# Second cross-attention: scores as 32-row tiles of one head instead of a block-diagonal query, and a BF16 one-hot spread in the expert layer

## The chip, the cores and the metric

The kernel runs on one core of a Trainium2 chip. A core has TensorE (matmuls into PSUM, eight banks of 512 fp32 columns), VectorE, ScalarE, GpSimd, and SyncE, whose queue here issues every DMA. The metric is device time in microseconds of one execution of the whole program, lower is better. TensorE's clock is granted by a throttle: 1.00 in the profile is 2.4 GHz, 0.50 is 1.2 GHz.

## What is computed

Two layers act on x (2 batches, 128 tokens, 128 features); each step is a layer norm, an operation and a residual. Layer 0 has a 16-head cross-attention on a context of 2048 keys, a latent attention and a top-1 expert layer of 8 experts; layer 1 a sparse cross-attention on the same context, a self-attention and a 16-expert layer. The change touches the expert layer of layer 0 and the cross-attention of layer 1:

```python
def _L0_ffn_ref(hidden_states, Wr, br, W1, W2):
    x = hidden_states.reshape(-1, h)
    route = jax.nn.sigmoid(x @ Wr + br)
    max_prob = jnp.max(route, axis=1, keepdims=True)
    max_ind = jnp.argmax(route, axis=1)
    for e in range(n_experts):
        mask = (max_ind == e)[:, None].astype(x.dtype)
        y = jax.nn.gelu(x @ W1[e], approximate=False) @ W2[e]
        out = out + mask * y
    out = out * max_prob

def _L1_xattn_ref(iQ, iK, mask, Wq, Wkv, Wo, nbias):
    rq = (iQ @ Wq.T).reshape(b, q, H, ADIM)          # 16 heads of 8
    kv = (iK @ Wkv.T).reshape(b, s, 2, H, ADIM)
    rk, rv = (kv[:, :, 0], kv[:, :, 1])
    scores = jnp.einsum('bqhd,bshd->bhqs', rq, rk) / sqrt(ADIM)
    scores = jnp.where(mask[:, None, :, :], jnp.float32(-1e+32), scores)
    t = jax.nn.relu(scores + nbias[0])
    t = t * t
    attn = t / (t.sum(-1, keepdims=True) + IEPS)
    o = jnp.einsum('bhqs,bshd->bqhd', attn, rv).reshape(b, q, H * ADIM)
    return o @ Wo.T
```

## The kernel before

Everything is written out by hand, engine by engine: each engine's program is a list of instructions in a fixed order, and semaphores tie the lists together. Names of semaphores say what is done (`mo_proj`: latent attention projected, `kstack_in[i]`: stacked keys of one group landed).

*Keys and values of layer 1* are projected early, in gaps: `fill(gap)` issues the items that `FILL` lists for a gap, "k" items (512 keys) and "v" items (four fp32 matmuls of 128 columns for 512 keys); ScalarE copies each out of its bank (`FILL_BANK`). fill(5), after the router's matmul, holds v1 to v7.

*Expert layer.* VectorE makes a one-hot of the chosen expert, then `diag`, 128x1024 per batch: identity times one-hot. TensorE multiplies xn with it (L889, four fp32 matmuls of 512 columns), which gives x laid out per expert with zeros elsewhere; ScalarE and VectorE copy that to `xm`. The up matmuls (L898, 4 x 8 of 256 columns) sum over experts in PSUM, ScalarE applies Gelu, the down matmuls (L906, 16 of 512 columns) give all experts' outputs, and VectorE picks with the one-hot. `keep_warm(4, 13)` then issues 13 matmuls of zeros while VectorE runs the layer norm.

*Scores of layer 1.* fp32r operands are split into a high and a low part. `kstack` holds, for each group g of four heads, 128 rows: 32 high, 32 low, 32 high again, and 32 rows of ones for the bias; SP copies these from `k1_hi` and `k1_lo` in 24 DMAs of 32 rows by 2048 keys (L565). q gets the matching rows in `q1s`, and `spread_q` multiplies it by `headsel` into `qbd`, block-diagonal: four heads side by side in 512 columns. A unit m is one block of 128 keys and 8 heads: two matmuls of 128 rows by 512 columns (L943) into two banks; three such slots rotate. A unit's scores wait only until the unit three before has been read out of its slot.

*The loop of 64 units.* Ten units (`SIDE`, every sixth) go to ScalarE (Relu, L1248) and GpSimd (mask L1410, square L1414). The other 54 go to VectorE (relu and mask, `w_ring`, L1642) and ScalarE (Square, `p_ring`, L1264). TensorE issues the scores of two units, then `weigh_v` of two older ones: 8 fp32 matmuls of 18 output rows each, in four column groups (L964). All units of a combo (batch, half of the heads) come one after another, 16 in a row; `copy_o1` takes a finished combo out of its bank.

An fp32 matmul stands as two instructions in the trace.

## Time and profile before

| | |
|---|---|
| three runs | 428.76, 432.27, 434.01 us (median 432.27) |
| the profiled execution | 429.39 us, its span 427.6 us, mean granted clock 0.992 |
| TensorE busy | 397.3 us, 93% of the span |
| VectorE, ScalarE, GpSimd busy | 330.1, 262.2, 230.5 us |
| chain that ended last | TensorE 76%, VectorE 9%, ScalarE 5%, issue 4%, DMA 3% |

The span lies 1.8 us under the execution's own time. The chain is read back from the last instruction, at each step to what released it, so an engine's share of the chain says where its time sets the end; its busy share doesn't.

### The profile page before, as it was taken

The page shows a single profiled execution, that of the slowest core. Times are in us where ns is not written, and L with a number is a line of the kernel's source. Part 1 is how long each engine was busy: PE and PEld are TensorE (multiplying, and loading weights), DVE is VectorE, ACT ScalarE, POOL GpSimd, SP SyncE. Part 2 cuts the span into 40 slices and gives each one's busy share as a digit, 9 for nine tenths or more (in the row PEclk, how much of TensorE's full clock was granted, in tenths as well). Part 3 has the DMA queues.
Part 4 walks back from the last instruction along what each step waited for, and adds up shares of the span by engine and source line. Part 5 has one row for each costly group of instructions (what it writes and reads, how often), then busy time and mean ns, then how long its engine had stood idle before and what let it go on. Part 6 is the DMA issues. An engine that isn't in the chain of part 4 may idle for free.

```text
span 427.6 us, 8049 instructions
## 1 busy us (share of the span) xinstructions
PE 397.3 (93%) x3128; PEld 322.9 (76%) x3128; DVE 330.1 (77%) x492; ACT 262.2 (61%) x384; POOL 230.5 (54%) x138
## 2 busy tenths in 40 slices
PE   8987999999999999999997979999799999976996
PEld 6765899999989899998995747755556666655795
DVE  4799888889888898885553845995798998952664
ACT  4477788787787877777542546100199989943343
POOL 0132799997879988775513100880097765500024
PEclk9999999999999999999999999999999999998999
DMA  7938877879998777777693007997000000010000
GB/s 224 287 97 200 195 173 173 187 179 199 228 214 181 174 177 178 178 173 174 227 423 124 2 0 159 222 211 313 0 2 3 2 2 3 2 34 0 2 0 15
DMA packets 20015, 57.06 MB, mean 133 GB/s; under 512 B 6528, under 2 KB 8104, under 8 KB 18312
## 3 DMA queue, kind: packets, MB, share of 16 engines
q1 hardware_dynamic: 19976, 56.53, 53.0%
q8 instruction: 25, 0.41, 0.4%
q14 instruction: 14, 0.11, 0.1%
HBM read 18.63 MB, written 0.13 MB: 44 GB/s over the span
## 4 chain that ended last, share of the span: by engine, by line
PE 76%; DVE 9%; ACT 5%; issue 4%; DMA 3%; POOL 1%; SPq 1%; POOLq 0%; ACTq 0%; DVEq 0%
PE ps L668 7%; PE ps L670 7%; PE ps L669 7%; PE ps L943 6%; PE ps L646 6%; PE ps L964 6%; PE ps L647 6%; PE ps L648 6%; PE ps L601 4%; PE ps L1037 3%; PE ps L898 3%; PE ps L906 3%; DVE max L1493 2%; PE ps L796 2%; DMA wkvo_sb<-in_wkvo 2%
## 5 line engine op out<-in xcount | busy, mean ns | idle before, releaser
L390 POOL TENSOR_TENSOR dT_lo<-z_sq,dT_hi 128x1024 fp32r<-128x1024 f32 x56 | 133.2, 2398 | 30.5 <-ACT dT_hi L1066 30.4
L1131 ACT ACTIVATE y_sq<-ps,nmax 128x1024 f32<-128x1024 f32 x64 | 70.8, 1112 | 40.1 <-DVE nmax L1522 38.6
L1493 DVE TENSOR_REDUCE max<-ps 128x1 f32<-128x1024 f32 x64 | 77.9, 1218 | 19.1 <-PE ps L648 19.1
L668 PE MATMUL ps<-dT_hi,ctx_hi 128*128 128x256 f32 x256 | 74.3, 290 | 1.3 <-POOL dT_lo L390 1.3
L1483 DVE STREAM_TRANSPOSE y_sq<-y_sq 128x1024 f32<-128x1024 f32 x60 | 74.0, 1234 | 0.0
L670 PE MATMUL ps<-dT_hi,ctx_lo 128*128 128x256 f32 x256 | 72.4, 283 | 0.0
L669 PE MATMUL ps<-dT_lo,ctx_hi 128*128 128x256 f32 x256 | 72.3, 283 | 0.0
L1642 DVE SCALAR_TENSOR_TENSOR w_ring<-ps,mask_sb 128x1024 f32<-128x1024 f32 x54 | 62.9, 1218 | 5.4 <-PE ps L943 4.3
L1066 ACT ACTIVATE dT_hi<-z_sq 128x1024 fp32r<-128x1024 f32 x60 | 61.5, 1059 | 2.7 <-PE ps L670 2.5
L1264 ACT ACTIVATE p_ring<-w_ring 128x1024 f32<-128x1024 f32 x54 | 55.8, 1055 | 4.3 <-DVE w_ring L1642 2.5
L646 PE MATMUL ps<-ctxT_hi,qk_hi 128*128 128x512 f32 x128 | 52.5, 410 | 4.0 <-ACT y_sq L1131 3.6
L668 PEld LDWEIGHTS ps<-dT_hi,ctx_hi 128*128 128x128 f32 x256 | 48.8, 191 | 3.9 <-issue 1.3
L647 PE MATMUL ps<-ctxT_hi,qk_lo 128*128 128x512 f32 x128 | 50.5, 394 | 0.0
L669 PEld LDWEIGHTS ps<-dT_lo,ctx_hi 128*128 128x128 f32 x256 | 48.9, 191 | 1.5
L648 PE MATMUL ps<-ctxT_lo,qk_hi 128*128 128x512 f32 x128 | 49.9, 390 | 0.0
L670 PEld LDWEIGHTS ps<-dT_hi,ctx_lo 128*128 128x128 f32 x256 | 48.8, 191 | 0.0
L943 PE MATMUL ps<-qbd,kstack 128*128 128x512 f32 x128 | 38.9, 423 | 2.5 <-DVE qbd L420 1.6
L1422 POOL TENSOR_TENSOR x<-x,y_scaled 128x128 f32<-128x128 f32 x17 | 7.7, 454 | 45.8 <-ACT y_scaled L1296 44.4
L964 PE MATMUL ps<-p_ring,v 128*18 128x128 f32 x864 | 30.2, 274 | 1.6 <-ACT p_ring L1264 1.5
L943 PEld LDWEIGHTS ps<-qbd,kstack 128*128 128x128 f32 x128 | 21.4, 188 | 13.5 <-DVE w_ring L1642 5.0
L646 PEld LDWEIGHTS ps<-ctxT_hi,qk_hi 128*128 128x128 f32 x128 | 24.2, 189 | 9.6 <-ACT y_sq L1131 4.6
L964 PEld LDWEIGHTS ps<-p_ring,v 128*18 128x18 f32 x864 | 20.6, 97 | 13.7 <-ACT p_ring L1264 11.7
(213 smaller groups left out, 646.0 us busy)
## 6 DMA issues: line engine op xcount, KB each, us to landing
z_sq<-y_sq SPq DMA_DIRECT2D x240, 128.0 KB, 2.4
w_sb<-in_w SPq DMA_DIRECT2D x2, 2048.0 KB, 14.3
kstack<-k_hi SPq DMA_DIRECT2D x16, 256.0 KB, 5.0
ctx_raw<-in_ctx_nat SPq DMA_DIRECT2D x8, 256.0 KB, 7.4
ctxT_raw<-in_ctx_t SPq DMA_DIRECT2D x1, 2048.0 KB, 8.0
kstack<-k_lo SPq DMA_DIRECT2D x8, 256.0 KB, 4.9
wg_sb<-in_wg SPq DMA_DIRECT2D x1, 1088.0 KB, 4.9
wu_sb<-in_wu SPq DMA_DIRECT2D x1, 1088.0 KB, 7.2
```

Source lines behind the costliest of these rows:

```text
L390: return engine.tensor_tensor(d_ring(dT_lo, m), z_chunk(m), d_ring(dT_hi, m), ALU.subtract)
L646: mm(acc, qk_hi[:, h, b, :], hi_t, start=True, stop=False)
L647: mm(acc, qk_lo[:, h, b, :], hi_t, start=False, stop=False)
L648: last = mm(acc, qk_hi[:, h, b, :], lo_t, start=False, stop=True)
L668: mm(acc, hi[:, k, :], dT_hi[m % 3][:, cols], start=(k == 0), stop=False)
L669: mm(acc, hi[:, k, :], dT_lo[m % 3][:, cols], start=False, stop=False)
L670: last = mm(acc, lo[:, k, :], dT_hi[m % 3][:, cols], start=False, stop=(k == NBLK - 1))
L943: last = mm(ps[:, 2 * (m % 3) + a, :], kstack[:, g, at:at + P], qbd[:, b, g, :, :].rearrange("p h s -> p (h s)"), start=True, stop=True)
L964: last = mm(ps[HR * j:HR * j + 2 * (DA + 1), 6 + c % 2, 0:S], v1[:, pair, a:a + 2, :].rearrange("p w d -> p (w d)"), p[:, (2 * j + a) * S: ...
L1131: nc.scalar.activation(out_t, keys, ACT.Exp, bias=nmax[:, hs % 2:hs % 2 + 1], scale=SCALE0, accum_out=rowsum[:, hs, p:p + 1]).then_inc(exp ...
L1483: v.transpose(y_half(hs, p), y_half(hs, p)).then_inc(squared, 1)
L1493: return v.tensor_reduce(max2[:, 2 * (hs % 2) + p:2 * (hs % 2) + p + 1], slot(2 * hs + p), AX.XY, ALU.max)
```

## The change

In the expert layer `diag` goes. GpSimd makes a BF16 identity early; TensorE spreads the BF16 one-hot over partitions with 16 matmuls of 128 columns (the stationary operand is one column of the one-hot, repeated), and VectorE multiplies the result with xnT into `xm`, two experts at a time; the up matmuls start per pair. Of the value projections v5 goes behind the up matmuls, v6 and v7 take the place of the 13 warming matmuls.

In the scores there is no block-diagonal query. `kstack` holds for each head 32 rows of its own: 8 high, 8 low, 8 high, 8 ones, so that four heads of a group fill the four row groups. A score matmul has 32 rows, 128 stationary keys and 128 columns of one head; for a block of keys 16 of them write four banks, row group r into bank r of a pair of slots. Two units (one block of keys, all 16 heads) are therefore one step, which waits for both slots. SP's copies become 8 rows by 2048 keys each: 24 for the ones (before, GpSimd wrote these with a memset), then 96 for the keys. q is projected batch by batch; VectorE makes the first batch's rows, GpSimd the second's. `SIDE` starts anew with each batch, and both combos of a batch run at once.

```diff
-        UNITS = NBLK
         COMBOS = B * 2
-        NU = COMBOS * UNITS
-        SIDE = tuple(range(0, NU - 6, 6))
+        NU = COMBOS * NBLK
+        SIDE = tuple(range(0, 25, 6)) + tuple(range(32, 57, 6))
...
-        FILL = (("k0", "k1", "k2"), ("k3",), ("k4",), ("v0",), ("k5", "k6", "k7"), tuple(f"v{i}" for i in range(1, NKV)))
+        FILL = (("k0", "k1", "k2"), ("k3",), ("k4",), ("v0",), ("k5", "k6", "k7"), ("v1", "v2", "v3", "v4"),
+                ("v5",), ("v6", "v7"))
         FILLS = [item for gap in FILL for item in gap]
-        FILL_BANK = dict(zip(FILLS, (6, 7, 4, 6, 7, 6, 7, 6, 2, 7, 6, 7, 6, 7, 6, 7)))
+        FILL_BANK = dict(zip(FILLS, (6, 7, 4, 6, 7, 6, 7, 6, 2, 7, 6, 7, 6, 4, 4, 4)))
...
-        def combo_weighed(c):
-
-            return max(weighed_nth(m) for m in range(c * UNITS, (c + 1) * UNITS))
+        def combo(m):
+
+            return m // (2 * NBLK) * 2 + m % 2
+
+        def block_of(m):
+
+            return m % (2 * NBLK) // 2
+
+        def of_combo(c):
+
+            return [weighed_nth(m) for m in range(NU) if combo(m) == c]
...
             sp.wait_ge(mo_proj, 1)
+            sp.wait_ge(ones_done, 1)
+            for b in range(B):
+                for g in range(3):
+                    keys = slice(b * CTX, (b + 1) * CTX)
+                    for r in range(4):
+                        rows = slice(HR * r + 3 * DA, HR * r + 4 * DA)
+                        sp.dma_start(kstack[rows, g, keys].bitcast(F32), kstack[rows, 3, keys].bitcast(F32))\
+                            .then_inc(ones_in[b], 16)
             sp.wait_ge(kv_act, FILLS.index("k7") + 1)
             sp.wait_ge(k1_split, NKV)
+
             for i in range(B * 4):
                 g, keys = i % 4, slice(i // 4 * CTX, (i // 4 + 1) * CTX)
-                for t in (0, 2, 1):
+                if g == 3:
+                    sp.wait_ge(ones_in[i // 4], 16 * 12)
+                for t in range(3):
                     part = k1_lo if t == 1 else k1_hi
-                    sp.dma_start(kstack[32 * t:32 * t + 32, g, keys].bitcast(F32),
-                                 part[32 * g:32 * g + 32, keys].bitcast(F32)).then_inc(kstack_in[i], 16)
+                    for r in range(4):
+                        sp.dma_start(kstack[HR * r + DA * t:HR * r + DA * t + DA, g, keys].bitcast(F32),
+                                     part[HR * r + DA * g:HR * r + DA * g + DA, keys].bitcast(F32))\
+                            .then_inc(kstack_in[i], 16)
 
             for i in range(B * 4):
-                sp.wait_ge(kstack_in[i], 48)
+                sp.wait_ge(kstack_in[i], 16 * 12)
+            sp.wait_ge(xn_ready, 4 * B)
             get(wg[:], "wg", "exp1")
             get(wu[:], "wu", "exp1")
             get(wd[:], "wd", "exp1")
...
-            for b in range(B):
-                pe.wait_ge(diag_done, b + 1)
-                for eh in range(2):
-                    mm(ps[:, 2 * b + eh, :], xn[:, b, :],
-                       diag[:, b, 4 * eh:4 * eh + 4, :].rearrange("p e s -> p (e s)"),
-                       start=True, stop=True).then_inc(xm_psum, 1)
+            pe.wait_ge(ident_done, 1)
+            pe.wait_ge(chosen, 1)
+            for e in range(E0):
+                for b in range(B):
+                    last = mm(ps[:, e // 2, (e % 2 * B + b) * S:(e % 2 * B + b + 1) * S],
+                              onehot[:, b, e:e + 1].to_broadcast([P, P]), ident_16[:], start=True, stop=True)
+                if e % 2:
+                    last.then_inc(picked, 1)
             pe.wait_ge(load["w1"], 16)
-            pe.wait_ge(xm_act, 2)
-            pe.wait_ge(xm_dve, 2)
-            pe.wait_ge(kv_act, 2 * NKV)
+            pe.wait_ge(kv_act, FILLS.index("v4") + 1)
             for f in range(NF):
                 for e in range(E0):
+                    if f == 0 and e % 2 == 0:
+                        pe.wait_ge(xm_done, e // 2 + 1)
                     last = mm(ps[:, 6 + f // 2, (f % 2) * T:(f % 2 + 1) * T], w1[:, e, f * P:(f + 1) * P],
-                              xm[:, :, e, :], start=(e == 0), stop=(e == E0 - 1))
+                              xm[:, e, :], start=(e == 0), stop=(e == E0 - 1))
                 last.then_inc(h0_psum, 1)
+            fill(6)
             pe.wait_ge(load["w2"], 16)
             pe.wait_ge(g0_done, NF)
             for b in range(B):
@@ -909,47 +935,50 @@
                     last.then_inc(y0_psum, 1)
 
 
-            keep_warm(4, 13)
-            pe.wait_ge(load["wq1"], 16)
+            fill(7)
+            pe.wait_ge(wq1_laid, 4)
             turn_xn(3)
-            for g in range(4):
-                last = mm(ps[:, 2 + g // 2 * 2, (g % 2) * T:(g % 2 + 1) * T], wq1[:, g, :], xnT[:],
-                          start=True, stop=True)
-                if g % 2:
-                    last.then_inc(q1_psum, 1)
+            for b in range(B):
+                for g in range(4):
+                    last = mm(ps[:, 2 + 2 * b, g * S:(g + 1) * S], wq1_rows[:, g, :], xnT[:, b * S:(b + 1) * S],
+                              start=True, stop=True)
+                last.then_inc(q1_psum, 1)
+
+            def slot_read(m):
+
+                if m in SIDE:
+                    pe.wait_ge(relu_done, side_nth(m))
+                else:
+                    pe.wait_ge(w1_done, main_nth(m))
 
             def scores1(m):
 
-                c, k = m // UNITS, m % UNITS
-                b = c // 2
-                if m >= 3:
-                    if m - 3 in SIDE:
-                        pe.wait_ge(relu_done, side_nth(m - 3))
-                    else:
-                        pe.wait_ge(w1_done, main_nth(m - 3))
-                if m == 0:
-                    pe.wait_ge(ones_done, 1)
+                b, k = m // (2 * NBLK), block_of(m)
+                for i in range(2):
+                    if m + i >= 3:
+                        slot_read(m + i - 3)
                 if m == 2:
-                    pe.wait_ge(q1s_done, 2)
-                for a in range(2):
-                    g = 2 * (c % 2) + a
+                    pe.wait_ge(q1b_read, 1)
+                if k == 0:
+                    pe.wait_ge(q_made[b], 1)
+                    pe.wait_ge(ones_in[b], 16 * 12)
+                at = b * CTX + k * P
+                for g in range(4):
                     if k == 0:
-                        if 4 * b + g >= 2:
-                            pe.wait_ge(qbd_pool, 4 * b + g - 1)
-                        else:
-                            pe.wait_ge(qbd_done, g + 1)
-                        pe.wait_ge(kstack_in[4 * b + g], 48)
-                    at = b * CTX + k * P
-                    last = mm(ps[:, 2 * (m % 3) + a, :], kstack[:, g, at:at + P],
-                              qbd[:, b, g, :, :].rearrange("p h s -> p (h s)"), start=True, stop=True)
-                last.then_inc(s1_psum, 1)
+                        pe.wait_ge(kstack_in[4 * b + g], 16 * 12)
+                    for r in range(4):
+                        rows, bank = slice(HR * r, HR * r + HR), 2 * ((m + r // 2) % 3) + r % 2
+                        last = mm(ps[:, bank, g * S:(g + 1) * S], kstack[rows, g, at:at + P], q_rows[rows, b, g, :],
+                                  start=True, stop=True)
+                        if g == 3 and r % 2:
+                            last.then_inc(s1_psum, 1)
 
             def weigh_v(m):
 
 
-                c, k = m // UNITS, m % UNITS
+                c, k = combo(m), block_of(m)
                 b, n = c // 2, weighed_nth(m)
-                first = n == min(weighed_nth(i) for i in range(c * UNITS, (c + 1) * UNITS))
+                first, final = n == min(of_combo(c)), n == max(of_combo(c))
                 if first and c >= 2:
                     pe.wait_ge(o1_copied, c - 1)
                 if m in SIDE:
@@ -964,15 +993,14 @@
                         last = mm(ps[HR * j:HR * j + 2 * (DA + 1), 6 + c % 2, 0:S],
                                   v1[:, pair, a:a + 2, :].rearrange("p w d -> p (w d)"),
                                   p[:, (2 * j + a) * S:(2 * j + a + 1) * S],
-                                  start=first and a == 0, stop=n == combo_weighed(c) and a == 1)
+                                  start=first and a == 0, stop=final and a == 1)
                 last.then_inc(pv1_done, 1)
 
             pe.wait_ge(acc_zero, 1)
             pe.wait_ge(zeroed, 4)
             for m in range(0, NU + WEIGH_LAG + 1, 2):
-                for i in range(2):
-                    if m + i < NU:
-                        scores1(m + i)
+                if m < NU:
+                    scores1(m)
                 for i in range(2):
                     if 0 <= m + i - WEIGH_LAG - 1 < NU:
                         weigh_v(WEIGHED[m + i - WEIGH_LAG - 1])
@@ -1225,18 +1253,20 @@
             act.wait_ge(rt_z, 1)
             nc.scalar.activation(rt[:, 1, :, :], rt[:, 0, :, :], ACT.Exp, scale=-1.0).then_inc(rt_e, 1)
             fill(5)
-            for i in range(2):
-                act.wait_ge(xm_psum, i + 1)
-                copy(xm[:, 0, 4 * i:4 * i + 4, :].rearrange("p e s -> p (e s)"), ps[:, i, :]).then_inc(xm_act, 1)
             for f in range(NF):
                 act.wait_ge(h0_psum, 2 * (f // 2) + 2)
                 nc.scalar.activation(g0[:, f, :], ps[:, 6 + f // 2, (f % 2) * T:(f % 2 + 1) * T],
                                      ACT.Gelu).then_inc(g0_done, 1)
 
 
+            fill(6)
+            fill(7)
             copy_xnT(3)
+            act.wait_ge(q1_psum, 2)
+            copy(q_raw[:].rearrange("p g s -> p (g s)"), ps[:, 4, :]).then_inc(q1b_read, 1)
...
-                if n + 3 < B * 4:
-                    spread_q(nc.gpsimd, n + 3).then_inc(qbd_pool, 1)
+                if n == 0:
+                    pool.wait_ge(q1b_read, 1)
+                    nc.gpsimd.tensor_scalar(q_high[:, 1, :, :], q_raw[:], SCALE1, None, ALU.mult).then_inc(q1b_part, 1)
+                    pool.wait_ge(q1b_part, 1)
+                    nc.gpsimd.tensor_scalar(q_part[:, 1, :, :], q_high[:, 1, :, :].bitcast(F32), q_signs[:, 1:2],
+                                            nb_rows[:], ALU.mult, ALU.add).then_inc(q1b_part, 1)
+                    nc.gpsimd.tensor_scalar(q_raw[:], q_raw[:], q_signs[:, 0:1], None, ALU.mult).then_inc(q1b_part, 1)
+                    pool.wait_ge(q1b_part, 3)
+                    nc.gpsimd.tensor_tensor(q_rows[:, 1, :, :], q_raw[:], q_part[:, 1, :, :], ALU.add)                        .then_inc(q_made[1], 1)
...
-            link(v.tensor_tensor(onehot, eq, bc(rtm[:, 1, :], 2, E0), ALU.is_equal))
-            for b in range(B):
-                v.tensor_tensor(diag[:, b, :, :], bc(ident[:], 1, E0), bc(onehot[:, b, :], 2, S), ALU.mult)\
-                    .then_inc(diag_done, 1)
-            link(v.tensor_tensor(eq, onehot, bc(rtm[:, 0, :], 2, E0), ALU.mult))
-            for i in range(2):
-                dve.wait_ge(xm_psum, 3 + i)
-                v.tensor_copy(xm[:, 1, 4 * i:4 * i + 4, :].rearrange("p e s -> p (e s)"), ps[:, 2 + i, :])\
-                    .then_inc(xm_dve, 1)
+            v.tensor_tensor(onehot[:], eq, bc(rtm[:, 1, :], 2, E0), ALU.is_equal).then_inc(chosen, 1)
+            for i in range(E0 // 2):
+                dve.wait_ge(picked, i + 1)
+                v.tensor_tensor(xm[:, 2 * i:2 * i + 2, :], ps[:, i, :].rearrange("p (e t) -> p e t", e=2),
+                                bc(xnT[:], 1, 2), ALU.mult).then_inc(xm_done, 1)
+            dve.wait_ge(chosen, 1)
+            link(v.tensor_tensor(eq, onehot[:], bc(rtm[:, 0, :], 2, E0), ALU.mult))
...
-            for i in range(2):
-                dve.wait_ge(q1_psum, i + 1)
-                q = q1s[:, 2 * i:2 * i + 2, :].rearrange("p g t -> p (g t)")
-                link(v.tensor_scalar(q[0:96, :], ps[0:96, 2 + 2 * i, :], SCALE1, None, ALU.mult))
-                v.scalar_tensor_tensor(q[64:96, :], ps[64:96, 2 + 2 * i, :], SCALE1, q[64:96, :], ALU.mult,
-                                       ALU.subtract).then_inc(q1s_done, 1)
-                dve.wait_ge(q1s_done, i + 1)
-                if i == 0:
-                    dve.wait_ge(nb_done, 6)
-                    spread_q(v, 0).then_inc(qbd_done, 1)
-                    spread_q(v, 1).then_inc(qbd_done, 1)
+            dve.wait_ge(q1_psum, 1)
+            dve.wait_ge(nb_done, 10)
+
+            def flat(t):
+                return t[:, 0, :, :].rearrange("p g s -> p (g s)")
+
+            link(v.tensor_scalar(flat(q_high), ps[:, 2, :], SCALE1, None, ALU.mult))
+            link(v.tensor_scalar(flat(q_part), flat(q_high), q_signs[:, 1:2], nb_rows[:], ALU.mult, ALU.add))
+            v.scalar_tensor_tensor(flat(q_rows), ps[:, 2, :], q_signs[:, 0:1], flat(q_part), ALU.mult, ALU.add)                .then_inc(q_made[0], 1)
```

TensorE from the last fill ahead of the expert layer to the first units of the loop, before (L796: value items, L889: spread, L898 and L906: up and down, L601: warming, L593: transposes of xn, L916: q, L943: scores, L964: weighing):

```order
L796 MATMUL ps<-wkvo_sb,ctxT_raw_149 128x128 x28
L889 MATMUL ps<-diag,xn 128x512 x4
L898 MATMUL ps<-xm,w_sb 128x256 x32
L906 MATMUL ps<-w_sb,g_151 128x512 x16
L601 MATMUL ps<-zeros 128x256 x13
L593 MATMUL ps<-ident_sb,xn 128x128 x2
L916 MATMUL ps<-xnT,wq_sb 128x256 x4
L943 MATMUL ps<-qbd,kstack 128x512 x12
L964 MATMUL ps<-p_ring,v_156 18x128 x16
```

Twelve of the 28 value matmuls will leave their place, and six units' scores are 12 matmuls. The same stretch of TensorE in the changed kernel (L819: value items, L913: spread of the one-hot, L923 and L932: up and down, L616: transposes, L943: q, L971: scores, L993: weighing):

```order
L819 MATMUL ps<-wkvo_sb,ctxT_raw_151 128x128 x16
L913 MATMUL ps<-ident_171,onehot 128x128 x16
L923 MATMUL ps<-xm,w_sb 128x256 x32
L819 MATMUL ps<-wkvo_sb,ctxT_raw_151 128x128 x4
L932 MATMUL ps<-w_sb,g_157 128x512 x16
L819 MATMUL ps<-wkvo_sb,ctxT_raw_151 128x128 x8
L616 MATMUL ps<-ident_sb,xn 128x128 x2
L943 MATMUL ps<-xnT,wq_rows 128x128 x8
L971 MATMUL ps<-q_rows,kstack 128x128 x48
L993 MATMUL ps<-p_ring,v_160 18x128 x16
```

Four value matmuls now stand behind the up matmuls and eight behind the down matmuls, the warming is gone, and the first six units' scores are 48 matmuls of 128 columns. SP's queue from the load of wq1 to the first weights of the last layer, before, where the last two rows stand eight times in all:

```order
L479 DMA wq_sb<-in_wq 128x512
L565 DMA kstack<-k_hi 32x2048 x2
L565 DMA kstack<-k_lo 32x2048
L565 DMA kstack<-k_hi 32x2048 x2
L565 DMA kstack<-k_lo 32x2048
```

And SP's queue in the changed kernel, from the same load on:

```order
L488 DMA wq_sb<-in_wq 128x512
L574 DMA kstack<-kstack 8x2048 x24
L586 DMA kstack<-k_hi 8x2048 x4
L586 DMA kstack<-k_lo 8x2048 x4
L586 DMA kstack<-k_hi 8x2048 x8
```

The ones (L574) stand first, and each group of keys that took three copies of 32 rows takes twelve of 8 rows (L586), 96 in all.

## Rows read from the trace of the kernel before

**Rows 1.** Chain of waits inside the loop: start us, length us, what.
```profile
335.98 1.00 PE ps L964 x32
336.98 1.12 PE ps L943 x4
...
376.16 1.22 DVE w_ring L1642
...
379.22 0.29 ACT oT L1066
```

**Rows 2.** Chain of waits from the latent attention to the loop.
```profile
239.10 1.65 PE ps L832 x30
...
252.79 0.44 DVE x L1577
...
257.58 6.59 PE ps L796 x56
264.17 3.45 PE ps L889 x8
267.65 0.70 DVE xm L1601
...
268.60 14.07 PE ps L898 x64
...
283.49 13.97 PE ps L906 x32
297.46 5.61 PE ps L601 x26
...
304.93 0.70 DVE q1s L1626
...
309.15 2.38 DVE w_ring L1642 x3
```

**Rows 3.** Groups by line in the loop: busy us, mean ns | idle before.
```profile
L1642 DVE SCALAR_TENSOR_TENSOR w_ring<-ps,mask_sb 128x1024 f32<-128x1024 f32 x54 | 62.9, 1218 | 5.4 <-PE ps L943 4.3 <-ACT p_ring L1264 0.5
L1264 ACT ACTIVATE p_ring<-w_ring 128x1024 f32<-128x1024 f32 x54 | 55.8, 1055 | 4.3 <-DVE w_ring L1642 2.5
...
L1248 ACT ACTIVATE w_side<-ps 128x1024 f32<-128x1024 f32 x10 | 10.1, 1009 | 4.6 <-PE ps L943 4.6
```

**Rows 4.** Timeline of SP's DMA issues: first key copies, first load behind them.
```profile
258.00 1.16 SPq L565 DMA_DIRECT2D kstack<-k_hi  x2
...
289.54 0.34 SPq L479 DMA_DIRECT2D wg_sb<-in_wg  x1
```

**Rows 5.** Timeline: latent scores, router, layer norm.
```profile
241.74 2.01 PEld L832 LDWEIGHTS ps<-qr,kr 16*128 16x128 f32 x32 [0.76 <-DVE clipped L1566]
...
242.95 2.36 DVE L1566 SCALAR_TENSOR_TENSOR clipped<-ps,causal 128x1024 f32<-128x1024 f32 x2 [0.22 <-PE ps L832]
...
259.59 0.17 DVE L1594 TENSOR_TENSOR rt<-rt,rtm 128x16 f32<-128x16 f32 x1
...
301.95 0.60 DVE L1455 TENSOR_SCALAR xn<-x,mv,nwt 128x128 f32<-128x128 f32 x2
```

**Rows 6.** GpSimd's memset of the ones, by its line: ns min/median/max.
```profile
L1399 POOL MEMSET kstack<- x1: 13812/13812/13812, 268.5 to 268.5; 32x16384 f32 x1
```

**Rows 7.** Busy time by stretch: PE, PEld, DVE, ACT, POOL, PEclk, DMA share, GB/s.
```profile
303.00:309.00 6.00, 3.66 (x15) 2.16 (x13) 3.93 (x6) 1.12 (x2) 0.00 (x0) 1.00 0.00 0
...
380.00:382.00 2.00, 0.64 (x4) 0.20 (x2) 0.97 (x3) 0.19 (x1) 0.00 (x0) 1.00 0.00 0
...
384.00:386.00 2.00, 2.00 (x7) 1.55 (x6) 1.76 (x12) 0.00 (x0) 0.00 (x0) 0.50 0.00 0
386.00:388.00 2.00, 1.53 (x8) 1.07 (x6) 0.31 (x2) 0.38 (x1) 0.00 (x0) 0.88 0.00 0
```

**Rows 8.** As rows 7: key copies, then the load of 128-row weights.
```profile
278.00:282.00 4.00, 4.00 (x20) 3.54 (x19) 4.00 (x2) 0.00 (x0) 4.00 (x1) 1.00 0.96 217
...
294.00:296.00 2.00, 2.00 (x6) 0.81 (x5) 1.80 (x3) 0.00 (x0) 0.00 (x0) 1.00 1.02 431
```

105 lines of the change are left out of this document (55 added, 50 removed).

## The prediction

> **What bounds the kernel now.** I read the chain of waits first, then the groups by line, then single stretches. In the second cross-attention the chain is TensorE without a break: 32 weighing instructions in 1.00 us, 4 score matmuls in 1.12 us, again and again [rows 1]. That is 2.13 us for a pair of units, and 32 pairs make the 68.2 us between VectorE's first unit at 309.15 [rows 2] and the end of its last at 377.38 [rows 1]. The reader is to see how little stands behind it: VectorE owes 54 x 1.218 = 65.8 us, ScalarE 54 x 1.055 + 10 x 1.009 = 67.1 us [rows 3]. A TensorE that needs nothing for the scores would save about 1 us here. Ahead of the loop, from 252.79 to 309.15, the chain is one long line through the expert layer and the making of q [rows 2]; there each piece taken off counts in full, as long as nothing else is late. The SP queue's copies of the stacked keys are not on that line: issued from 258.00, all landed by 289.54 [rows 4], 20 us early.
>
> **The expert layer.** fill(5) held seven value projections, 6.59 us, 0.94 each [rows 2]; four stay, so TensorE is through at 261.35. The one-hot has been ready since 259.76 [rows 5]. Removed are the four spreading matmuls, 3.45 us, the copy, 0.70, and the 0.25 us between its end and the first up matmul [rows 2]. Added are 16 BF16 matmuls and four VectorE products. No row shows a BF16 matmul of 128 columns: four of them cost at least nothing and at most 4 x 0.12 (6.59 / 56) plus a latency of 0.3; I take 0.5, near the upper end, and keep 0.3 to 0.8. The first product lasts 0.70 like the copy it resembles, and the expert matmuls start near 262.65 instead of 268.60. Later products (0.72 apart) stay ahead of TensorE, which needs 14.07 / 16 = 0.88 us for two experts [rows 2]. Gain 5.95 us, 2.8 of it the three projections moved away.
> Those three are paid where TensorE waited anyway: one in the 0.82 us before the down matmuls (+0.12), two behind these in place of 26 keep-warm instructions of 5.61 us [rows 2]. That filler lasted longer than the layer norm it covered: xn was done at 302.55, 5.09 us after the last down matmul, while the transposes stood behind the filler's end at 303.07 [rows 2, 5]. Now the down matmuls end at 291.63, xn is done at 296.72 and the transposes follow 0.05 later, so the gain is 6.3.
> GpSimd's work is costed at nothing: its memset shrinks from 16384 to 4096 columns, 13.8 us to some 3.5 [rows 6] and stands before any work of the expert layer; the ones are wanted at 252.8. The four strided copies of wq1 start with the end of the up matmuls (276.7) under 14 us of down matmuls. Without that cover each would add about half a microsecond.
>
> **Making q.** The first batch's projection is half as much work per step, but before, too, VectorE waited for its first half only, so it stays: VectorE starts on q at 304.93 - 6.3 = 298.63. It then makes three passes of 0.70 [rows 2] with 0.06 between, instead of two passes, two spreads and two passes: the first scores may start at 300.85, and VectorE's first unit follows L later (L below, 0.86): 301.7 against 309.15. **Gain ahead of the loop: 7.4 us.** The second batch's q is made by GpSimd behind its first side unit and has 36 us of time.
>
> **The loop.** A pair's scores are now 16 matmuls of 32 rows, four row groups into four banks. The nearest rows are the 16-row score tiles of the latent attention, in two row groups: the first weight load at 241.74, the consumer at 242.95 after 16 instructions [rows 5], and 1.65 us for 30 [rows 2], so a pace of 0.05 us and a fixed 0.46. Four column groups run at 1.00 / 32 = 0.031 [rows 1]. With four row groups I take 0.031; the even unit of a pair is done at the 14th matmul, so L = 13 x 0.031 + 0.46 = 0.86; bounds 0.46 (all side by side) and 1.11 (0.05 each, no better than two groups).
> The Trainium skill ("TensorE: Matmul & The Clock Gate", Part 3) has four row tiles start some 4 ns apart; by that L would be about 0.5 and the sum below 3.6 us better. The 0.031 [rows 1] speaks against so small a step, though there the groups are columns.
> TensorE then needs no more than 1.00 + 0.86 = 1.86 us a pair and bounds nothing. But the wait is tighter: the three bank slots are freed one unit at a time, and a pair now starts only when both of its slots are free, where each unit started alone. So at each of the ten side units a chain closes: ScalarE's Square of the unit before (1.055), its Relu of the side unit (1.01), the next pair's scores (L), three VectorE units (3 x 1.22), and 0.11 of semaphores: 5.84 + L for six units. At L = 0.86 this is 6.70 us where TensorE took 3 x 2.13 = 6.39. Ten such chains, less the first Square (1.1), plus the five units outside them (6.1): 63.4 + 10 L = 72.0 us, against 68.2. **Loss 3.8 us** (bounds -0.2 and +6.3). The two copies at the half-way point and one more at the end (0.29 each [rows 1]) add 0.6.
>
> **The clock.** With the filler gone TensorE has from 292.6 to 297.5 one projection and two transposes. A stretch of that kind stands later: after 380 to 382 with 0.64 us busy in 2, the granted clock fell to 0.50 (1.2 GHz) and was back after some 3.5 us [rows 7]. Here it would double 1.2 us of transposes and projection: +1.2, bounds 0 and 3.
>
> **The keys' copies.** This is the term I know least. 24 copies of 32 rows become 24 + 96 of 8 rows with rows as long as before (8 KB), all on SP; the ones go first, and behind them the first batch's 48. They start at 252.9 (x is updated at 252.79 [rows 2], the ones are ready). 72 must have landed by 300.85: break-even is 48 / 72 = 0.67 us each. One old copy took 31.54 / 24 = 1.31 us [rows 4]. Low end: the same bytes per second, 0.33 us. High end: a copy costs what its 8 KB row costs, 1.31. For the middle: 128-row loads move 431 GB/s, these 32-row copies 217 with the DMA share near 1.0 in both [rows 8]; a quarter of the rows halved the rate, and a second halving gives 0.66 us. I take 0.66: 72 land at 300.4, just in time, all 120 at 332.1, where the second half asks for them at 337. Cost 0, but with no margin: each 0.1 us more costs 7.2 us.
>
> **Sum** on the profiled execution (429.39 us, span 427.6): -7.4 + 3.8 + 0.6 + 1.2 + 0 = -1.8, so 427.6. The median of the three runs lies 2.9 above that execution; I forecast 430 on its scale. Some 2%, 8.6 us, is what a measurement of this kernel can tell from no change.
>
> **Rivals.**
> *The copies are late.* The price per copy stays nearer to 1.31 because the rate goes with the rows touched. For it: the halving [rows 8]. Against: the share stays 1.0, so the engines, not the rows, may have been the limit. At 0.79 the first batch is 8.9 us late and the second 1.6 more, and the change is 2% slower: that is where this rival decides. At 1.0: +24.0 + 11.7, 463; at 1.31: +46.4 + 26.6, 501.
> The Trainium skill ("SBUF — State Buffer", Door 1) says bandwidth goes with the SBUF ports that the partitions reach: 32 partitions 8 ports, 8 consecutive ones 2, of 27.2 GB/s each; 54 GB/s would be 1.2 us a copy and a time near 487. The trace agrees for 32 rows (217 of its 218 GB/s), which is why the chance below is not small.
> *The scores start early and the chain is short.* L at 0.46, no fall of the clock: -7.4 - 0.2 + 0.6, 422 there, 425 on the median. If ScalarE also runs without a gap, the loop is its 67.1, which is 0.9 less, and with picks at 0.3 the time is just over 2% below the median.
> *The tiles don't run side by side*: L 1.11, +2.5, 430 there. It ends within the forecast's range.
> *The clock stays at half in the loop* because TensorE now rests a sixth of it: 2 x 1.86 us a pair, 119 us for 72, about 475. Against it: 303 to 309, 61% busy, held 1.00 [rows 7].
>
> **How the numbers follow.** Copies in time or nearly so, 424 to 434: 45 in 100. Copies at 0.70 to 0.79, up to 2% slower: 11. Copies later: 30. Clock: 4. Faster by over 2%: 10. So faster 0.10, same 0.56, slower 0.34. The range runs from 423 to 460: about 5 are left out below, 15 above (copies over 0.95 us). The forecast's own range is 424 to 434.
>
> **What would show it.** After: expert matmuls from 262.7, down matmuls to 291.6, scores from 300.9 with no idle time before them that a key copy ends; a pair's 16 score matmuls in 0.5 to 0.8 us; ScalarE's and VectorE's groups in the loop unchanged in duration and TensorE waiting for them; a loop of some 72 us; a clock dip around 297. What would make it wrong: SP's copies at over 0.7 us each (then TensorE's longest wait is for them, at the loop's start and again half way), a chain at the side units shorter than 5.84 + L because ScalarE runs ahead, or a clock that doesn't return.

## The result

The changed kernel takes 448.71 us (median of four runs, 444.97 to 451.83), the kernel before 432.49 on the same terms (428.76 to 434.01). The ratio is 1.036, with a 95% interval of 1.026 to 1.046: slower by some 16 us. I had forecast no change beyond 2%, and had named the mechanism that won, late key copies, as a rival. Ratios, here and below, leave out executions that ran over 1.5% longer than the fastest of their kernel, while medians and ranges count all.

The profiled execution has a span of 446.3 us against 427.6, 18.7 more. The chain of waits of the changed kernel from the latent attention on (start us, length us, what) says where it went:

```profile
254.10 0.72 SPq L574
...
273.09 1.20 SPq L574
...
274.39 0.62 SPq L586
...
352.49 0.79 SPq L586
353.32 4.94 DMA kstack<-k_hi
358.30 0.48 PE ps L971 x3
358.78 1.84 PE ps L993 x32
360.62 1.11 PE ps L971 x15
```

What used to be TensorE, VectorE and ScalarE [rows 2] is now SP's queue alone, one DMA issue after another for 99 us: the 24 copies of ones (L574) and the 96 key copies (L586). From 254.10 to 353.32 that is 0.827 us a copy, and the last lands 4.94 us after its issue ends. The rest of the program runs beside it and waits for it twice. TensorE's and VectorE's timelines of the changed kernel (start us, busy us, what, idle before it and its releaser) show both stops and VectorE's first and last units:

```profile
302.54 0.44 PE L971 MATMUL ps<-q_rows,kstack 32*128 32x128 f32 x8 [0.60 <-issue]
309.66 0.48 PE L971 MATMUL ps<-q_rows,kstack 32*128 32x128 f32 x4 [6.68 <-DMA kstack<-k_hi]
320.05 0.48 PE L971 MATMUL ps<-q_rows,kstack 32*128 32x128 f32 x4 [9.90 <-DMA kstack<-k_hi]
...
358.30 0.48 PE L971 MATMUL ps<-q_rows,kstack 32*128 32x128 f32 x4 [1.69 <-DMA kstack<-k_hi]
...
320.67 1.23 DVE L1679 SCALAR_TENSOR_TENSOR w_ring<-ps,mask_sb 128x1024 f32<-128x1024 f32 x1 [18.35 <-PE ps L971]
...
391.06 6.88 DVE L1679 SCALAR_TENSOR_TENSOR w_ring<-ps,mask_sb 128x1024 f32<-128x1024 f32 x6 [0.58 <-PE ps L971]
```

The first scores could start at 302.54 and were complete at 320.5. VectorE's first unit began at 320.67 instead of 309.15 (+11.5; 1.3 of it had passed when x was updated, at 254.10 instead of 252.79). Its last unit began 76.0 us after its first, where it was 67.0 before [rows 1, 2] (+9.0): the new loop takes 4.2 us longer even when the copies are in time (run 3), and the rest is the second stop at 358 and the clock after it, below. What follows the loop was 1.8 us shorter. Together 18.7.

The groups by line show that VectorE's and ScalarE's instructions of the loop got no slower (busy us, mean ns, idle before it):

```profile
L1679 DVE SCALAR_TENSOR_TENSOR w_ring<-ps,mask_sb 128x1024 f32<-128x1024 f32 x54 | 62.8, 1219 | 32.8 <-PE ps L971 32.8
L1295 ACT ACTIVATE p_ring<-w_ring 128x1024 f32<-128x1024 f32 x54 | 56.1, 1057 | 9.9 <-DVE w_ring L1679 7.2
```

1219 and 1057 ns against 1218 and 1055 [rows 3]; what grew is the idle time ahead of them, from 5.4 to 32.8 us and from 4.3 to 9.9. The stretches of the changed kernel (length, then busy time of PE, PEld, DVE, ACT, POOL, then granted clock, DMA share, GB/s):

```profile
276.00:296.00 20.00, 18.66 (x65) 10.31 (x63) 9.14 (x18) 2.49 (x5) 2.06 (x4) 1.00 0.51 80
...
320.00:328.00 8.00, 5.44 (x84) 4.34 (x84) 5.93 (x5) 5.27 (x5) 6.00 (x4) 0.50 0.53 82
...
360.00:364.00 4.00, 4.00 (x72) 2.85 (x64) 2.37 (x3) 2.76 (x3) 3.92 (x2) 0.50 0.97 394
```

The copies move 80 GB/s with a DMA share of 0.51, where 32-row copies moved 217 at 0.96 [rows 8]. And after both stops TensorE was granted half its clock (0.50, 1.2 GHz): a pair of units took 1.84 + 1.11 us there, as the chain shows at 358.78.

### The profile page after: what moved, and what is told of

Read it like the earlier page. It is cut to its first block, busy times and chain, and to the rows that moved or that the text cites. A ratio compares the mean times of both kernels' runs of the same rounds, so it can differ in the third digit from the quotient of the medians.

```text
span 446.3 us, 8920 instructions
## 1 busy us (share of the span) xinstructions
PE 384.1 (86%) x3502; PEld 320.0 (72%) x3502; DVE 312.0 (70%) x489; ACT 263.0 (59%) x383; POOL 217.9 (49%) x145
## 4 chain that ended last, share of the span: by engine, by line
PE 49%; SPq 24%; DVE 9%; DMA 7%; ACT 5%; issue 4%; POOL 1%; POOLq 0%; ACTq 0%; DVEq 0%
SPq L586 17%; PE ps L691 6%; PE ps L692 6%; PE ps L693 6%; PE ps L669 5%; PE ps L670 5%; PE ps L671 5%; SPq L574 4%; PE ps L1065 3%; DMA ctx_raw<-in_ctx_nat 3%; DVE max L1534 3%; PE ps L993 3%; DVE w_ring L1679 2%; DVE y_sq L1524 2%; DMA wkvo_sb<-in_wkvo 2%
## 5 line engine op out<-in xcount | busy, mean ns | idle before, releaser
L1534 DVE TENSOR_REDUCE max<-ps 128x1 f32<-128x1024 f32 x64 | 78.0, 1218 | 20.0 <-PE ps L671 20.0
L1679 DVE SCALAR_TENSOR_TENSOR w_ring<-ps,mask_sb 128x1024 f32<-128x1024 f32 x54 | 62.8, 1219 | 32.8 <-PE ps L971 32.8
L1295 ACT ACTIVATE p_ring<-w_ring 128x1024 f32<-128x1024 f32 x54 | 56.1, 1057 | 9.9 <-DVE w_ring L1679 7.2
L1444 POOL TENSOR_TENSOR w_side<-w_side,cap_side 128x1024 f32<-128x1024 f32 x10 | 21.4, 2142 | 66.3 <-ACT w_side L1278 66.3
L971 PE MATMUL ps<-q_rows,kstack 32*128 32x128 f32 x512 | 26.4, 322 | 30.1 <-DMA kstack<-k_hi 18.3
L691 PEld LDWEIGHTS ps<-dT_hi,ctx_hi 128*128 128x128 f32 x256 | 48.8, 191 | 4.9 <-issue 2.3
L971 PEld LDWEIGHTS ps<-q_rows,kstack 32*128 32x128 f32 x512 | 21.5, 220 | 39.7 <-DMA kstack<-k_hi 18.7
L693 PEld LDWEIGHTS ps<-dT_hi,ctx_lo 128*128 128x128 f32 x256 | 48.8, 191 | 0.0
L993 PE MATMUL ps<-p_ring,v 128*18 128x128 f32 x864 | 35.0, 306 | 3.1 <-ACT p_ring L1295 2.1
L993 PEld LDWEIGHTS ps<-p_ring,v 128*18 128x18 f32 x864 | 22.5, 107 | 8.9 <-ACT p_ring L1295 3.8
```

What stands on the lines that cost most here:

```text
L691: mm(acc, hi[:, k, :], dT_hi[m % 3][:, cols], start=(k == 0), stop=False)
L693: last = mm(acc, lo[:, k, :], dT_hi[m % 3][:, cols], start=False, stop=(k == NBLK - 1))
L1534: return v.tensor_reduce(max2[:, 2 * (hs % 2) + p:2 * (hs % 2) + p + 1], slot(2 * hs + p), AX.XY, ALU.max)
L1679: v.scalar_tensor_tensor(w_ring[:, (at - 1) % 3, :].rearrange("p (h s) -> p h s", h=8), ps[:, bank:bank + 2, :].rearrange("p a (h s) -> p ...
```

## The experiments

Each was run beside the kernel before; ratios are to it, with 95% intervals. "First unit" and "last unit" give when VectorE's first and last units of the loop start; "the loop" is the time between them, 67.0 us before. Traces are of one execution each. The moment at which x is updated, before the changed part, differs among them by up to 3.4 us (252.79 before, 256.20 in run 5, 253.66 in run 8, whose code up to there is that of run 5), so short gains are read from that moment on.

**1. The ones without SP's queue.**

```diff
-                        sp.dma_start(kstack[rows, g, keys].bitcast(F32), kstack[rows, 3, keys].bitcast(F32))\
-                            .then_inc(ones_in[b], 16)
...
+            pool.wait_ge(mo_proj, 1)
+            for b in range(B):
+                for g in range(3):
+                    nc.gpsimd.memset(kstack[:, g, b * CTX:(b + 1) * CTX].bitcast(F32), 1.0).then_inc(ones_done, 1)
```

The key copies wait for these memsets instead.

> Only the 24 copies of ones leave SP's queue: GpSimd writes the ones itself with six memsets of 2048 columns after the latent attention, and the 96 key copies keep their form. Theory (the copies set both starts of the loop, at 0.83 us each as in the changed kernel): key copies run from 258 on, 48 are issued by 298 and landed by 303, all 96 issued by 338 and landed by 343, so the first scores that feed VectorE end near 303 instead of 320, the second half starts near 343 instead of 358, and the span falls by 15 to 19 us, to 427 to 431. Rival (the loop itself is slow, from its shared waits or from the clock): the start moves but the loop keeps some 78 us, and the span stays over 432. Rival (the price is paid per time and not per copy, something else holds the queue): no change.

439.45 us, ratio 1.018 (1.013 to 1.022): 9 us better than the change, span 438.8 instead of 427 to 431. The second half started at 348.5 instead of 358.3 and no copy stood ahead of the first scores, so the direction held. The size didn't, and what came is what the first rival had named, a loop of 78.4 us and a span over 432. But the second half still waited for a copy inside that loop, so the run doesn't tell a slow loop from late copies; runs 3 and 5 do. TensorE's timeline there:

```profile
348.48 0.48 PE L961 MATMUL ps<-q_rows,kstack 32*128 32x128 f32 x4 [5.26 <-DMA kstack<-k_hi]
```

Part of the lateness was of my own making. VectorE's and GpSimd's timeline in this kernel:

```profile
254.17 10.74 POOL L1427 MEMSET kstack<- 128x2048 f32 x6 [10.26 <-PE ps L887]
...
256.03 1.73 DVE L1480 TENSOR_SCALAR nwt<-nwt 128x2 int32<-128x2 int32 x1
```

VectorE's tiny step of the layer norm took 1.73 us, one memset long, where it takes 0.17 in the changed kernel; with its like and the split of the keys behind it, SP's key copies began at 261.59 instead of the 258 expected, and the first scores at 306.80 instead of 302.54.

**2. The new expert layer alone**, with the old scores, old copies and the old loop (edit: the expert layer's part of the diff on the kernel before).

> The kernel before with the new expert layer alone (one-hot spread, products, fills moved, no warming matmuls); scores, key copies of 32 rows and the loop are those of before. Theory: the gain that the prediction worked out ahead of the loop counts in full where the copies are early, 6.3 us, less up to 1.2 if the clock dips: 424 to 428 on the median of before, ratio 0.982 to 0.99. Rival (the expert layer's gain was never there, since something else is late ahead of the loop): ratio 1.00.

424.81 us, ratio 0.984 (0.981 to 0.987): faster, as worked out. First unit at 306.0, last at 373.0, so the old loop of 67.0. From x's update to the first unit it took 50.9 us where it took 56.4 before: 5.5 of the 6.3 forecast, with the clock at 0.86 and 0.72 from 296 to 304.

**3. Rows four partitions apart.**

```diff
-    sp.dma_start(kstack[HR * r + DA * t:HR * r + DA * t + DA, g, keys].bitcast(F32),
-                 part[HR * r + DA * g:HR * r + DA * g + DA, keys].bitcast(F32))
+    sp.dma_start(kstack[HR * r + t:HR * r + HR:4, g, keys].bitcast(F32),
+                 part[HR * r + g:HR * r + HR:4, keys].bitcast(F32))
```

and the ones likewise.

> The changed kernel with the 8 rows of each copy four partitions apart (over 32 partitions) instead of next to each other, at both ends; count, bytes and queue are the same. The key rows then meet the wrong rows of q, so the scores are not the reference's. If the price comes from 8 neighbouring partitions being reached through few ports, the copies get faster, 0.62 us (the shortest issue seen) or less, the first scores are complete near 305 and the span is under 435. If it comes from 8 rows being served by half of the DMA engines (share 0.52), the pace stays at 0.80 to 0.85 and the span at 444 to 448.

426.97 us in a single run, span 425.1, against a median of 431.76 for the kernel before. Number of copies, bytes and queue are the same, and some 21 us are gone from the span. SP's timeline in this kernel, with the last key copies and the first load that waits for all of them:

```profile
270.21 2.97 SPq L586 DMA_DIRECT2D kstack<-k_hi  x4
273.22 2.63 SPq L586 DMA_DIRECT2D kstack<-k_lo  x4
...
333.57 2.62 SPq L586 DMA_DIRECT2D kstack<-k_hi  x4
337.68 0.34 SPq L488 DMA_DIRECT2D wg_sb<-in_wg  x1
```

2.63 / 4 = 0.66 us a copy is now the queue's own pace (0.685 over all 120), the last copies land 1.5 us behind their issue, and TensorE waits for a copy once, for 0.5 us. In the stretch from 276 to 296:

```profile
276.00:296.00 20.00, 18.58 (x64) 10.23 (x63) 9.20 (x19) 2.51 (x5) 2.06 (x4) 1.00 0.26 99
```

more bytes a second with half the DMA time of the changed kernel (share 0.26 for 0.51). The rival, 8 rows served by half of the DMA engines, would have kept the pace at 0.80 to 0.85. So the partitions that a copy touches set the pace, until the queue's issue does.

**4. Zeros into the two waits**, to keep the clock.

```diff
                 at = b * CTX + k * P
+                if k == 0:
+                    keep_warm(2 * (m % 3), 5 if b else 38)
```

> The changed kernel with matmuls of zeros in TensorE's two waits for the copies (38 ahead of the first batch's scores, 5 ahead of the second's); nothing else. Theory (copies set both starts, the fall of the clock costs only after them): starts stay at 320 and 358; the first pairs take some 2.1 us instead of 2.9, which the second wait hides, and those after 358 too, which counts: 3 to 4 us less than the changed kernel, 441 to 446, still slower than before. Rival (the clock is the main cause): within 2% of before, 440 or less. Rival (the clock costs nothing): as the changed kernel, 446 to 450.

The four executions took 448.79, 456.07, 457.28 and 461.42 us. The theory's 441 to 446 didn't come in any, and they lie too far apart to tell its 3 to 4 us. The profiled one is the longest, so its total isn't compared. Its stretches:

```profile
316.00:320.00 4.00, 4.00 (x20) 3.54 (x19) 0.00 (x0) 0.00 (x0) 0.00 (x0) 1.00 0.54 76
...
332.00:336.00 4.00, 4.00 (x72) 2.85 (x64) 3.46 (x4) 3.15 (x3) 3.92 (x2) 0.50 0.50 68
```

After a dip to 0.50 from 300 to 304 the clock was at 1.00 from 308 to 324, through the filled wait, and then fell in the loop all the same. What the clock costs the changed kernel is left open by this run.

**5. Rows apart, made right**, on the changed kernel: the projection's columns, q's rows and the signs follow, GpSimd writes the ones after the expert products, and the first batch's copies wait for its own keys only.

> The changed kernel computing the reference with key rows four partitions apart (q's rows, the projection's columns and the signs follow), the ones written by GpSimd only after the expert products, and the first batch's copies not held for the second batch's keys. Theory (the copies' pace was all that made the change slower): 96 copies at 0.66 us end near 330, no wait of TensorE for a copy is left, the first scores end near 303, and the time is 422 to 427, faster than before. Rival (the loop with two units a step has a loss of its own, as rows-apart showed: 72.5 us from VectorE's first unit to the end of its last, where before took 68.2): 424 to 429, no better than the new expert layer alone (424.8), although the scores start 2 to 3 us earlier than there.

430.77 us, ratio 0.997 (0.993 to 1.000). TensorE has no wait for a copy left, first unit at 305.9, last at 377.3: 71.4 us, 4.4 more than the old loop. The theory's 422 to 427 is missed and the rival is right in kind, though its 424 to 429 is still low: the copies' pace was not all. With them in time the new scores give back what the expert layer gains.

**6 and 7. One side apart**: only the rows written, then only the rows read.

> Like rows-apart, but only the rows written are four partitions apart; the rows read stay next to each other (scores again not the reference's). If what limits a copy is the writing side, the pace is near 0.66 us and the span near 425; if it is the reading side, 0.80 to 0.85 and 444 to 448; if both count alike, the slower one still sets it: 444 to 448 here and in the mirror run.

> The mirror: only the rows read are four partitions apart, the rows written stay next to each other (scores not the reference's). Reading side limits: pace near 0.66, span near 425. Writing side or both alike: 0.80 to 0.85, 444 to 448.

451.03 and 472.65 us, a single run each: neighbouring rows on either side are enough to keep the copies slow, and the two show up in different places. SP's timeline with only the written rows apart (run 6):

```profile
352.24 3.72 SPq L586 DMA_DIRECT2D kstack<-k_hi  x4
359.08 0.34 SPq L488 DMA_DIRECT2D wg_sb<-in_wg  x1
```

and with only the rows read apart (run 7):

```profile
332.20 2.78 SPq L586 DMA_DIRECT2D kstack<-k_hi  x4
376.82 0.34 SPq L488 DMA_DIRECT2D wg_sb<-in_wg  x1
```

Slow reading (run 6) holds the queue up: issues end at 355.96, 0.85 us each, the load behind them follows 3.1 us later. Slow writing (run 7) doesn't: issues run at 0.66 us to 334.98, and the data comes in until 376.8, 42 us behind, at 64 GB/s. My expectation of the second run, 444 to 448, was too low by 23; why writing alone is slower than both sides together isn't settled.

**8. Zeros ahead of the loop**, on run 5's kernel: `keep_warm(5, 4)` before the transposes of xn, `keep_warm(5, 2)` after the projection of q.

> As the first kernel of this call, with 4 matmuls of zeros while VectorE makes xn and 2 behind the projection of q. Theory (the granted clock falls to 0.50 at the loop's start because TensorE rests from 295 to 303, and that costs the first pairs 2 to 3 us): the clock holds 1.00 to 312 and the time is 1 to 3 us less than the first kernel's. Rival (the clock falls in the loop's own ramp, where the first steps wait for VectorE): no difference, or up to 1 us more for the six matmuls.

429.88 us, ratio 0.991 (0.988 to 0.995). From x's update the first unit came 0.9 us sooner than in run 5 (48.8 for 49.7), and the loop was 1.1 longer (72.5). The medians are 0.9 apart, at the low end of the theory's 1 to 3, but its reason failed. From 300 to 304 the clock held 1.00, where it was 0.57 in run 5; from 304 on it fell all the same (0.92 and 0.50 in run 5):

```profile
300.00:304.00 4.00, 2.30 (x38) 1.64 (x36) 2.52 (x3) 1.95 (x3) 0.53 (x1) 1.00 0.25 96
304.00:308.00 4.00, 2.59 (x52) 2.18 (x48) 3.75 (x4) 2.98 (x4) 3.84 (x3) 0.59 0.25 100
308.00:312.00 4.00, 4.00 (x72) 2.91 (x64) 2.18 (x2) 3.42 (x4) 3.81 (x4) 0.50 0.27 100
```

**9. A wait for each unit** in place of the shared one, on run 8's kernel.

```diff
-                for i in range(2):
-                    if m + i >= 3:
-                        slot_read(m + i - 3)
...
+                for i in range(2):
+                    if m + i >= 3:
+                        slot_read(m + i - 3)
+                    for g in range(4):
...
+                        for r in (2 * i, 2 * i + 1):
```

> The warmed rows-apart kernel, but a step's scores come in two halves: 8 matmuls of the first unit (row groups 0 and 1) wait for the first slot alone, 8 of the second (row groups 2 and 3) for the second slot. Theory (the wait for both slots together is what the loop of the new scores loses, 73.5 to 75 us against 69.3 from VectorE's first unit to ScalarE's last Square): six units take 6.28 us (ScalarE's own 5 x 1.055 + 1.01) instead of 6.34 and the first steps follow closer, 2 to 3 us less in all, 426 to 428. Rival (the loss lies in the half-way point, where both combos end at once, and in the clock): within 1 us of the warmed kernel, 429 to 431.

426.60 us, ratio 0.990 (0.984 to 0.996), from which alone run 8's kernel can't be told apart. The traces can. Six units of the second half with the shared wait, from run 8's TensorE:

```profile
355.83 0.67 PE L964 MATMUL ps<-q_rows,kstack 32*128 32x128 f32 x16 [0.34 <-ACT w_side L1271]
...
362.17 0.67 PE L964 MATMUL ps<-q_rows,kstack 32*128 32x128 f32 x16 [0.34 <-ACT w_side L1271]
```

and with the wait for each unit:

```profile
355.31 0.69 PE L964 MATMUL ps<-q_rows,kstack 32*128 32x128 f32 x16
...
361.23 0.69 PE L964 MATMUL ps<-q_rows,kstack 32*128 32x128 f32 x16
```

6.34 us against 5.92. That is also less than the 6.28 that I took for ScalarE's floor: by the timeline ScalarE's five Squares of a turn take 5.12 us in a row (from 353.21), 1.02 each, though one lasts 1.053 on average, and six of VectorE's units in a row take 6.88, 1.147 each, though one lasts 1.217. Durations overlap, so a floor made of them is too high. From one side unit's Relu to the next (352.30 to 358.23) ScalarE doesn't rest there: 5.92 is its own pace. The loop went from 72.5 us (302.4 to 374.9) to 68.4 (302.9 to 371.3). The chain of this kernel then shows a stop of another kind:

```profile
312.09 1.29 POOL q_rows L1453
313.37 2.11 POOL w_side L1440
315.55 1.91 POOL p_side L1444
317.75 0.71 issue
```

GpSimd's work on the second batch's q stands ahead of the second side unit.

**10. Zeros in the first three steps**, on run 8's kernel: three matmuls more behind the scores of each.

> The warmed rows-apart kernel with 3 more matmuls of zeros behind the scores of each of the first three steps, where TensorE waits for VectorE. Theory (the granted clock falls to 0.50 at 305 because TensorE rests in the first steps, and that lasts 9 us): it holds 1.00 through 302 to 320 and the time is 1.5 to 3 us less than the warmed kernel's 429.9. Rival (the fall at 305 comes from the rest before 302 and can't be mended there, or costs nothing since VectorE and ScalarE set the pace): no difference.

432.53 us, ratio 1.001 (0.997 to 1.004): not better. The clock did hold through the start, and fell later, from a stretch (320 to 324) in which TensorE was busy for 2.27 of 4 us; in run 5 it was busy for 2.41 there and no fall followed:

```profile
304.00:308.00 4.00, 3.40 (x42) 2.48 (x41) 2.39 (x3) 2.10 (x3) 0.68 (x1) 1.00 0.26 98
...
324.00:328.00 4.00, 3.95 (x88) 2.94 (x84) 3.31 (x4) 2.97 (x3) 2.11 (x2) 0.68 0.28 102
...
340.00:344.00 4.00, 4.00 (x80) 3.10 (x80) 2.92 (x4) 3.15 (x4) 1.61 (x1) 0.54 0.00 0
```

**11. The expert layer alone with zeros while VectorE makes xn** (`keep_warm(5, 4)` on run 2's kernel).

> The new expert layer with the old scores, and 4 matmuls of zeros while VectorE makes xn. Theory (the granted clock was 0.86 and 0.72 from 296 to 304 there; transposes, projection of q and the first scores stand on the chain): 0.5 to 1.5 us less than the new expert layer alone (424.8), the fastest version of this study. Rival (the four matmuls end after xn is ready, or VectorE's chain hides the clock): 424.5 to 425.5.

424.82 us, ratio 0.984 (0.979 to 0.989): the same as run 2. The clock held 1.00 where it had been 0.86 and 0.72, and the first unit came 49.8 us after x's update instead of 50.9, as the theory had it. The medians don't show this 1 us.

**12. GpSimd's q in four pieces**, one behind each of its first four side units, on run 9's kernel.

> The kernel with unit waits, but GpSimd makes the second batch's q in four pieces, one behind each of its first four side units, instead of all behind the first. Theory (in the kernel with unit waits VectorE and ScalarE stood from 315 to 319 because the second side unit waited for GpSimd's 5 us on q): that wait goes, the loop from VectorE's first unit to the end of ScalarE's last Square takes 67 to 68.5 us instead of 70.7, and the time is 2 to 3 us less than with unit waits: 0.982 to 0.986 of before, level with the new expert layer and the old scores (0.984) or just under it. Rival (the stop was the clock's, 0.64 from 320 to 324, and GpSimd was only near): the loop stays at 70 to 71 us and the ratio at 0.99.

426.82 us (421.62 to 428.21), ratio 0.985 (0.979 to 0.992). The stop of run 9 is gone from the chain, but the loop has the same length, 68.5 us (304.6 to 373.1; to the end of ScalarE's last Square, as the expectation counts, 70.8 for 70.7). In its profiled execution the clock lay at half at both starts:

```profile
308.00:312.00 4.00, 4.00 (x76) 3.07 (x72) 3.48 (x4) 3.39 (x5) 3.33 (x3) 0.50 0.26 102
...
348.00:352.00 4.00, 4.00 (x72) 3.16 (x76) 2.43 (x3) 2.67 (x4) 2.32 (x2) 0.53 0.02 4
```

So the loop's length met the rival's number and the ratio met the theory's; the run settles neither. This and the expert layer alone (runs 2 and 11) are the fastest versions, level with each other: even mended, the new scores add nothing to the new expert layer.

## Why the prediction was wrong

**The step that failed is the keys' copies**: "I take 0.66: 72 land at 300.4, just in time ... Cost 0, but with no margin". Three of its numbers were off on the same side. The pace was 0.827 us a copy, over the 0.79 from which the rival decides: 72 x (0.827 - 0.67) = 11.3 us. The issue of the first batch's last copy ended at 313.85 and TensorE's wait for it at 320.05; I had let a copy land as it was issued, and it takes 5 to 6.2 us more. And the start slid with the program, 254.10 for 252.9. Together the scores were complete some 18 us after q was ready. The second batch, forecast to land at 332.1, landed at 358.3, and the second half began with it. At 0.827 the rival's own sum gives 427.6 + 11.3 + 3.8 = 442.7 us, an estimate that lacks the landing time, where the profiled execution took 448.24.

The reason I gave for 0.66, that a quarter of the rows had halved the rate and another quarter would halve it again, has no ground in the runs; that spread rows do run at 0.66 is chance, for that is the queue's issue. What counts is which partitions a copy reaches, at both ends: with eight rows spread over 32 partitions at both ends the changed kernel runs in 426.97 us (run 3), with either end close together in 451.03 or 472.65 (runs 6, 7). The Trainium skill ("SBUF — State Buffer", Door 1) has DMA bandwidth go with the number of SBUF ports that the partitions reach, which I had weighed as a rival and then given too little; the trace agrees, and shows it at each end. The estimate from its 27.2 GB/s a port, 54 GB/s for the two ports of eight neighbouring partitions, is too low here: the runs moved 80, and 64 in the worst case. But that estimate is for one copy, and here several were under way at once to different partitions, one issued every 0.83 us and landing 5 us later; so the runs don't test it for a copy alone.

**What was right.** *The expert layer*: forecast 6.3 us ahead of q. In the changed kernel the up matmuls started 9.65 us after x was updated (263.75 from 254.10), forecast 9.86; the sixteen BF16 picks took 1.26 us from their first to the first up matmul, of which I had 0.5 for the first four and 0.70 for a product. By itself the expert layer is worth 1.6% (run 2). In the changed kernel it bought nothing, since q waited 18 us for keys. The timeline of the changed kernel's TensorE through this layer:

```profile
258.75 3.90 PE L819 MATMUL ps<-wkvo_sb,ctxT_raw 128*128 128x128 f32 x32
262.49 1.06 PE L913 MATMUL ps<-ident,onehot 128*128 128x128 bf16 x16
263.75 14.05 PE L923 MATMUL ps<-xm,w_sb 128*128 128x256 f32 x64 [0.20 <-DVE xm L1638]
```

*Making q*: first scores forecast at 300.85, 48.1 us after x; they came at 302.54, 48.4 after it.

*The loop*: forecast 3.8 us longer; with the copies out of the way it is 4.2 longer (run 3: first unit 304.4, last 375.6). The sum came out for partly wrong reasons. The chain at the side units exists, and taking the shared wait away shows it (run 9: 0.42 us in six units, some 4 over the loop), but it costs 6.34 us a turn and not 6.70. The difference went into things that I had at 0.6 or at nothing. In run 3 the first turn, at half the clock, takes 7.65 us, the second, behind GpSimd's q, 7.16, and the one over the half-way point 8.68: there both combos end at once, TensorE stands 1.79 us for their copies and the clock falls to 0.73. How each turn's excess divides among these isn't shown.

*TensorE's room*: a pair's scores take 0.67 us at full clock (forecast 0.5 to 0.8), VectorE follows their start by 0.70 (L, forecast 0.86), and TensorE no longer bounds the loop. With the shared wait that is worth next to nothing, 6.34 us for six units where TensorE took 3 x 2.13 = 6.39 [rows 1]. I had put what VectorE and ScalarE leave at 1 us for the whole loop; run 9 shows more, 0.47 in six units, because my floors added durations that overlap. It came to nothing there too, since the two starts and the half-way point took it back (68.4 us against 67.0).

**The clock** was mis-sized: a dip of 1.2 us around 297 was forecast and came (0.88 and 0.69 from 296 to 304), but the larger part came with the stops: 0.50 from 308, in the first wait, to 328, and from 360 to 372. I had priced the copies' lateness without it. Run 4 doesn't tell what it cost, but other numbers on record bound it. At the first stop it cost the end nothing, for the second half began when the last copy had landed, at 358.3, and SP's queue doesn't wait for TensorE. From ScalarE's first side unit of the second half to the end of VectorE's last unit the changed kernel took 39.1 us (358.82 to 397.94); runs 3, 5 and 8, whose copies were in time, took 36.4 each (from 340.35, 342.08 and 339.67), with a shorter fall of the clock. By this difference the second fall is worth at most some 2.7 of the 18.7 us; it is read from one execution each, and that nothing else behind the stop adds to it isn't shown.

## What to carry to other kernels

- A transfer between partitions is priced by the partitions it touches on both sides, not by its bytes or rows alone, and a queue of short ones by its issue (0.66 us a copy here). Before cutting one 32-row copy into four of eight neighbouring rows, lay the rows out so that each copy still spans the 32.
- A term with "cost 0 but no margin" that falls due at a known moment is a coin toss, and belongs in the forecast at half of its range; count the time from issue to landing in it.
- When an edit makes an engine's work shorter, look at what it does to that engine's waits (two slots for one here) before counting the saved instructions.

## What the runs showed of the hardware

- Reading and writing are slow in different ways. With neighbouring rows on the reading side, issues on SP's queue stretch (0.85 us each in run 6); on the writing side the queue issues on at 0.66 and the data lags up to 42 us behind (run 7). A queue that issues freely says nothing about when data lands.
- A GpSimd memset of 2048 columns held up a VectorE instruction of 128x2 elements for its whole length (1.73 us for 0.17, run 1). The Trainium skill has it ("SBUF — State Buffer", SBUF: two separate sides): GpSimd and some of VectorE's instructions share a port pair under an exclusive lock, held for a whole instruction. The trace agrees: the wait is one memset long, 10.74 / 6 = 1.79 us, and only VectorE's TENSOR_SCALARs were held (0.65, 1.73 and 1.37 us); SCALAR_TENSOR_TENSORs of 128x2 between them took 0.15 to 0.16.
- Filling TensorE's rests with zeros moved the fall of its clock and didn't remove it with the new scores (runs 4, 8, 10); with the old ones it did (run 11). In the profiled executions of the kernels with the old scores (before, runs 2 and 11) the clock stayed at 1.00 through the loop; TensorE worked there almost without a rest.
